# Two heads' context keys and values projected early, an inverse transform with two matrices, and a norm moved to ScalarE

## The chip, the core and the metric

The program runs on one core of one Trainium2 chip. A core has five engines that run at once, each with its own queue of instructions, and wait for each other by semaphores: TensorE (PE in the profile; its weight loads are PEld), VectorE (DVE), ScalarE (ACT), GpSimd (POOL) and SyncE (SP, which here only issues DMAs). The metric is the device time of one execution in microseconds (us); lower is better.

## What is computed

A decoder of two layers in fp32 on x of 8 batches x 128 tokens x 512 features, with a context of the same shape. Each of six steps adds to x and is followed by a layer norm. The steps that the change touches, cut to what matters:

```python
def _autocorrelation(Q=x, K=ctx, V=ctx):        # 8 heads of 64, L = 128
    corr = ifft(fft(q) * conj(fft(k))).real     # along the tokens, for each column
    w, idx = top_k(corr, 9); w = softmax(w)
    for i in range(9):
        g = minimum(idx[..., i] + pos, L - 1)   # shifted values, the last one repeated
        out = out + w[..., i] * take_along_axis(v, g)

def _L1_xattn_ref(latents=x, context=ctx, ...): # 32 query heads, 8 key heads of 128
    kv = concatenate([context, latents], axis=1)
    q = rms_norm(latents @ Wq); k = rms_norm(kv @ Wk); v = kv @ Wv
    out = softmax(q @ k.T / sqrt(128)) @ v
    return out @ Wo

x = _layernorm(x + _L0_attn_ref(x, w1, w2, b2, mask))      # masked dense, gelu
x = _layernorm(x + _autocorrelation(x, ctx, ctx))
x = _layernorm(x + _L0_ffn_ref(x, ...))                     # base product and routed adapters
x = _layernorm(x + _L1_attn_ref(x, ...))                    # state space mixer, 8 groups
x = _layernorm(x + _L1_xattn_ref(x, ctx, ...))              # cross attention
x = _layernorm(x + _L1_ffn_ref(x, ...))                     # product with adapters
```

## The kernel before, in words

x stays in SBUF as eight tiles of 128 x 512, one for each batch. Large products are made in three passes (`three_pass`, L269 to L273): each operand is split into a rounded high part, written by ACT (`..._hi`), and the rest, written by DVE or POOL (`..._lo`), and PE adds high x high, low x high and high x low. The order of the instructions on each engine is written out by hand; nothing is scheduled by a planner. All times below are from the start of the span.

**Masked dense, 0 to 58 us** (`stage_masked_dense`, L282). PE takes the batches in a row. Each goes on through DVE (bias, L366), ACT (gelu, L334), POOL (sum into x, L348), DVE (norm statistics), POOL (`norm_rstd`, L233 and L235) and DVE (`norm_apply`, L241). A barrier ends the stage.

**Autocorrelation, 58 to 190 us** (class `Autocorrelation`; its order on each engine stands in `stage_routed_mixer`). For batch b PE turns the weights of the nine taps (`turn_weights`, L540), waits for ACT's copy, transforms them (`transform`, L548 and L549), makes the correlation of batch b + 2 (`correlate`, L522, L523), the transforms of the values of b + 1 (`values`, L532, L533), turns x of b - 2 (L251), makes the inverse transform (`out`, L565: four full fp32 products, one for each of the four tiles that DVE made in `products`, L695) and the spectra of b + 3 (`spectra`, L508 to L514). DVE makes the four products and then picks the nine taps of b + 1 (`pick`, L649 to L679, which ends with `b_weights`). After the output of batch 5 PE goes on with `routed.base(0)`, the first product of the next stage, which needs the low parts `c_w_lo` that POOL makes at L627, one of four slices in each of the batches 2 to 5, behind that batch's `norm_rstd`.

**Routed product, to about 262 us**, then the **mixer** to about 1660 us.

**Cross attention, 1660 to 2510 us** (`stage_cross_attention`, L1760). Its 64 units are 8 key heads x 8 batches (unit n: head n // 8, batch n % 8). In one round PE does `attend(n)`, `turn_q(n+2)`, `project_kv(n+3)`, `turn_probs(n+1)`, `score(n+2)`, `project_q(n+3)`, `turn_k(n+3)` and `out(n)`. `project_kv` makes keys and values of one head together, 256 columns: 12 passes over the context (high and low parts `e_ctx_hi`, `e_ctx_lo`) and 12 over x (`XH`, `XL`). ACT evacuates them (`evac_kv`, L2055 and L2059), splits the turned probabilities (L2092), makes the exponentials (L2084), and in the rounds whose n % 8 is 0 to 3 it rounds two weights of the next head (L182) before it copies the output (L2097) and the turned queries (L2077). The last step is a product with adapters, to the end.

## Time and profile before

| what | value |
|---|---|
| median of 3 runs | 2551.83 us (2551.8 to 2552.94) |
| the profiled execution's own time | 2551.84 us |
| its span, first to last instruction | 2550.1 us |
| PE busy over the span | 2477.9 us (97%) |
| PE busy, 58 to 186 us | 113.82 of 128 us, granted clock 0.94 |
| PE busy, 1700 to 2400 us | 700 of 700 us, granted clock 1.00 |
| DVE, ACT, POOL busy, 1900 to 2000 us | 66.60, 58.15, 25.47 us |
| granted clock of PE, 156 to 161 us | 0.50 |
| DMA share of 16 engines, 1900 to 2000 us | 0.10 |

Busy is the time in which an engine works on an instruction; matmuls overlap, so the time from the start of one to the start of the next is what one costs. The granted clock is a share of full speed (1.00 is 2.4 GHz, 0.50 is 1.2 GHz). What an engine waits for stands in brackets behind an instruction in the trace.

### The profile page before, as it was taken

What the parts mean: (1) busy time and instruction counts of PE and PEld (TensorE: products, weight loads), DVE (VectorE), ACT (ScalarE), POOL (GpSimd) and SP (SyncE); (2) the same over time, 40 slices, a digit from 0 to 9 for tenths busy, and PEclk for the clock granted to TensorE, in tenths of its full rate; (3) what the DMA queues carried; (4) which work ended last, traced back from release to release, by engine and by line L of the source; (5) the groups of instructions that cost most, each with busy time, mean ns of one, the idle gap of its engine ahead of it and who ended that gap; (6) DMA issues with size and microseconds to landing.
All of it is one profiled execution on the core that took longest, in us unless ns stands there. A gap on an engine that the chain in (4) does not pass through costs nothing. (4 is left out here: it accounts for less than half of the span.)

```text
span 2550.1 us, 39113 instructions
## 1 busy us (share of the span) xinstructions
PE 2477.9 (97%) x14056; PEld 2033.2 (80%) x14056; DVE 1866.3 (73%) x2530; ACT 1122.6 (44%) x2660; POOL 1082.3 (42%) x890
## 2 busy tenths in 40 slices
PE   7989899999999999999999999899999999999999
PEld 4547788888888888888888887788888888888886
DVE  4877986886977968859869678656666666666675
ACT  2323343343443443433434433455656556555551
POOL 3012655645655655556566555632312223222123
PEclk8999999999999999999999999999999999999999
DMA  4000420321412303313213131110101001000100
GB/s 151 28 1 9 164 101 30 144 95 54 145 42 91 120 29 120 116 38 136 71 64 139 38 116 64 60 42 26 34 18 34 26 17 42 16 27 26 56 3 34
DMA packets 61554, 163.82 MB, mean 64 GB/s; under 512 B 8336, under 2 KB 8976, under 8 KB 52944
## 3 DMA queue, kind: packets, MB, share of 16 engines
q1 hardware_dynamic: 60144, 159.21, 18.2%
q8 instruction: 113, 1.85, 0.3%
q10 hardware_dynamic: 1248, 2.36, 0.3%
q14 instruction: 49, 0.40, 0.1%
HBM read 158.92 MB, written 2.62 MB: 63 GB/s over the span
## 5 line engine op out<-in xcount | busy, mean ns | idle before, releaser
L271 PE MATMUL pair<-XH,d_w_hi 128*128 128x512 f32 x1160 | 471.8, 407 | 2.8 <-DVE d_gated L1633 1.7
L272 PE MATMUL pair<-XL,d_w_hi 128*128 128x512 f32 x1160 | 460.3, 397 | 0.0
L273 PE MATMUL pair<-XH,d_w_lo 128*128 128x512 f32 x1160 | 459.7, 396 | 0.0
L1492 POOL TENSOR_TENSOR d_decay<-d_decay,d_cb 128x1024 f32<-128x1024 f32 x128 | 311.1, 2431 | 137.2 <-DVE d_decay L1610 137.2
L1610 DVE TENSOR_TENSOR_SCAN d_decay<-d_decay,m_delta 128x1024 f32<-128x1024 f32 x128 | 363.5, 2841 | 1.5 <-DVE d_dtg L1578 1.5
L1473 POOL TENSOR_TENSOR d_w_lo<-d_w,d_w_hi 128x512 fp32r<-128x512 f32 x144 | 188.6, 1312 | 268.1 <-ACT d_w_hi L1313 267.4
L271 PEld LDWEIGHTS pair<-XH,d_w_hi 128*128 128x128 f32 x1160 | 218.8, 189 | 60.1 <-issue 12.8
L1595 DVE SCALAR_TENSOR_TENSOR d_hs<-pair,d_conv,d_hs 128x1016 f32<-128x1016 f32 (+2 forms) x192 | 242.9, 1265 | 29.2 <-ACT d_hs L1338 24.7
L273 PEld LDWEIGHTS pair<-XH,d_w_lo 128*128 128x128 f32 x1160 | 218.7, 189 | 52.9
L272 PEld LDWEIGHTS pair<-XL,d_w_hi 128*128 128x128 f32 x1160 | 219.0, 189 | 47.1
L1497 POOL TENSOR_TENSOR d_gated_lo<-d_gated,d_gated_hi 128x512 fp32r<-128x512 f32 x128 | 173.4, 1357 | 159.1 <-ACT d_gated_hi L1357 159.1
L1338 ACT ACTIVATE d_hs<-pair,d_conv 128x1024 f32<-128x1024 f32 x64 | 77.1, 1205 | 357.0 <-PE pair L273 357.0
L2084 ACT ACTIVATE e_probs<-pair,e_nm,e_rq 128x256 f32<-128x256 f32 x256 | 141.1, 562 | 175.5 <-DVE e_nm L2289 175.5
L271 PE MATMUL pair<-d_wo_hi,d_gated_hi 128*128 128x512 f32 x512 | 207.4, 405 | 7.9 <-POOL d_gated_lo L1497 7.9
L273 PE MATMUL pair<-d_wo_hi,d_gated_lo 128*128 128x512 f32 x512 | 201.3, 393 | 0.0
L272 PE MATMUL pair<-d_wo_lo,d_gated_hi 128*128 128x512 f32 x512 | 199.7, 390 | 0.0
L2188 POOL TENSOR_TENSOR e_rq<-e_rq,mhalf 128x4 f32<-128x4 f32 x64 | 64.7, 1010 | 268.6 <-DVE e_rq L2271 268.6
L1357 ACT ACTIVATE d_gated_hi<-d_gated 128x512 fp32r<-128x512 f32 x128 | 80.0, 631 | 218.2 <-PE pair L273 197.1
L1638 DVE TENSOR_REDUCE d_sq_sum<-d_xdt 128x128 f32<-128x1024 f32 x64 | 128.3, 2005 | 63.2 <-ACT d_xdt L1364 63.2
L1345 ACT ACTIVATE d_hs<-d_hs 128x1024 f32<-128x1024 f32 x64 | 67.7, 1058 | 161.0 <-DVE d_hs L1595 161.0
L1192 PEld LDWEIGHTS pair<-d_decay,d_xdt 128*64 128x64 f32 x2048 | 112.1, 138 | 28.3 <-issue 28.3
L1192 PE MATMUL pair<-d_decay,d_xdt 128*64 128x128 f32 x2048 | 127.6, 278 | 5.2 <-POOL d_decay L1492 5.2
(280 smaller groups left out, 6032.4 us busy)
## 6 DMA issues: line engine op xcount, KB each, us to landing
d_decay<-token_decays SPq DMA_DIRECT2D x64, 1024.0 KB, 4.9
d_w<-in_L_w_groups SPq DMA_DIRECT2D x144, 256.0 KB, 2.7
e_w<-in_L_w_heads SPq DMA_DIRECT2D x80, 256.0 KB, 2.7
d_wo<-in_L_wo_groups SPq DMA_DIRECT2D x64, 256.0 KB, 4.9
X<-in_x SPq DMA_DIRECT2D x8, 256.0 KB, 10.3
b_ctx<-in_ctx SPq DMA_DIRECT2D x8, 256.0 KB, 12.0
e_ctx<-in_ctx_t SPq DMA_DIRECT2D x4, 512.0 KB, 6.5
out<-X SPq DMA_DIRECT2D x8, 256.0 KB, 2.0
```

The source lines that it names most:

```text
L271: pe.matmul(out, wh, xh, start=first, stop=False)
L272: pe.matmul(out, wh, xl, start=False, stop=False)
L273: return pe.matmul(out, wl, xh, start=False, stop=last)
L1192: last = pe.matmul(Y[e * PM:(e + 1) * PM, b * S:(b + 1) * S], XDT[:, b, e * PM:(e + 1) * PM], R[:, j % RSLOT, e, b * S:(b + 1) * S], start ...
L1357: act.activation(GH[:, x, :, :], GT[:, 4 * x:4 * x + 4, b * S:(b + 1) * S], ACT.Copy).then_inc(q["g_hi"], 1)
L1473: pool.tensor_tensor(WL[:, w, :, :], WR[:, w, :, :], WH[:, w, :, :].bitcast(F32), ALU.subtract).then_inc(q["w_split"], 1)
L1492: pool.tensor_tensor(r, r, GM_[:], ALU.mult).then_inc(q["scores"], 1)
L1497: pool.tensor_tensor(GL[:, x, :, :], GT[:, 4 * x:4 * x + 4, b * S:(b + 1) * S], GH[:, x, :, :].bitcast(F32), ALU.subtract).then_inc(q["g_l ...
L1595: v.scalar_tensor_tensor(dst[:, :, back:], src[:, :, :S - back], PC[:, n, KM - 1 - back:KM - back], dst[:, :, back:], ALU.mult, ALU.add).t ...
L1610: v.tensor_tensor_scan(r, r, m["DELTA"][:], 0.0, ALU.mult, ALU.add).then_inc(q["decay"], 1)
L1638: v.tensor_reduce(SQS[:, b % 2, :], SQ[:].rearrange("p j t -> p t j"), AX.X, ALU.add)\
L2084: act.activation(PR[:, n % 2, h, :], score_bank(h), ACT.Exp, bias=NM[:, n % 2, h:h + 1], scale=RQ[:, n % 2, h:h + 1], accum_out=SUM[:, n % ...
```

## The change

It does six things.

1. A class `KeysAhead` projects context keys and values of the heads 2 and 5 before the attention, in eight items of two batches (a half of an item is one batch: 12 passes of 256 columns). Items 0 and 1 (head 2, batches 0 to 3) stand on PE behind the last batch of the masked dense stage, item 2 behind `values(0)` of the autocorrelation, and the items 3 to 7 at its batches 0, 2, 3, 4 and 5: one half ahead of `turn_weights`, the other between it and `transform`. Weights and context (2.5 MB) are loaded in the first stage; ACT and POOL split them; ACT copies each item out of PSUM, and SP stores it to DRAM.
2. In the attention the 16 units of these heads leave out the 12 passes over the context. ACT issues two DMAs of 64 KB one unit ahead for each; the copy of the values, their low part and the scaling of the keys become two instructions of 128 columns where one of 256 stood.
3. `out` makes two products where it made four: POOL adds the first two of DVE's tiles and subtracts the last two (`parts`), and ACT writes a third copy of the values with its row 0 replaced (two instructions more in `values_copied`).
4. The norm of the autocorrelation is applied by ACT (`shifted`), with a shift that POOL makes, and no more by DVE.
5. The four slices of `c_w_hi` and `c_w_lo` are made two in each of the batches 2 and 3.
6. Tiles move: the products to the area of the mixer's weights, so that SP loads the first of these once the last `out` is done (it did so at the stage's start); the routed product's small tiles to another area.

```diff
 # stage_masked_dense: SP, ACT, POOL, PE
+                keys.weights(sp, 0)
+                keys.context(sp)
                 sp.wait_ge(next_in, 16 * (1 + NB))
+                for i in range(2):
+                    keys.store(sp, i)
...
+                    if b == 1:
+                        keys.w_hi(act, 0)
+                    if 2 <= b < 6:
+                        keys.c_hi(act, b - 2)
+                for i in range(2):
+                    keys.copy(act, i)
+                    for b in (2 * i + 4, 2 * i + 5):
+                        keys.c_hi(act, b)
...
                     if b:
                         norm_rstd(c, pool, s, b - 1)
+                    if b == 1:
+                        keys.w_lo(pool, 0)
+                    if 2 <= b < 6:
+                        keys.c_lo(pool, b - 2)
...
+                pe.wait_ge(first.lo, NB)
+                for i in range(2):
+                    for half in range(2):
+                        keys.project(pe, i, half)
 # Autocorrelation
     def out(self, pe, b):
-        for i in range(4):
-            pe.wait_ge(q["products"], 4 * b + i + 1)
-            last = pe.matmul(c.bank[7][:, :], f(M_AA + i), self.PR[:, i, :], start=i == 0, stop=i == 3)
+        for i in range(2):
+            pe.wait_ge(q["parts"], 2 * b + i + 1)
+            last = pe.matmul(c.bank[7][:, :], f(M_A + i), self.PT[:, i, :], start=i == 0, stop=i == 1)
...
     def values_copied(self, act, b):
+        act.activation(self.AV[:], c.bank[1][:, :], ACT.Copy).then_inc(q["uf_copied"], 1)
+        act.activation(self.AX[:], c.bank[1][:, :], ACT.Copy).then_inc(q["uf_copied"], 1)
+        act.activation(self.BV[:], c.bank[2][:, :], ACT.Copy, scale=self.REST[:, 0:1]).then_inc(q["uf_copied"], 1)
+        act.activation(self.AX[0:1, :], c.bank[2][0:1, :], ACT.Copy, scale=-1.0).then_inc(q["uf_copied"], 1)
+    def shifted(self, act, b):
+        act.activation(self.c.X[:, b, :], self.c.X[:, b, :], ACT.Identity, bias=self.SHIFT[:, b:b + 1],
+                       scale=self.c.rstd[:, b, :]).then_inc(self.s.normed, 1)
...
-        if b in (2, 3, 4, 5):
-            act.activation(nxt["WH"][:, b - 2, :], nxt["W"][:, b - 2, :], ACT.Copy).then_inc(q["next_hi"], 1)
+        for k in {2: (0, 1), 3: (2, 3)}.get(b, ()):
+            act.activation(nxt["WH"][:, k, :], nxt["W"][:, k, :], ACT.Copy).then_inc(q["next_hi"], 1)
+    def parts(self, pool, b):
+        for i, op in enumerate((ALU.add, ALU.subtract)):
+            pool.wait_ge(q["products"], 4 * b + 2 * i + 2)
+            pool.tensor_tensor(self.PT[:, i, :], self.PR[:, 2 * i, :], self.PR[:, 2 * i + 1, :], op).then_inc(q["parts"], 1)
 # stage_routed_mixer: PE, ACT, POOL
+                    item = {0: 3, 2: 4, 3: 5, 4: 6, 5: 7}.get(b)
+                    if item is not None:
+                        keys.project(pe, item, 0)
                     auto.turn_weights(pe, b)
+                    if item is not None:
+                        keys.project(pe, item, 1)
                     auto.transform(pe, b)
...
+                    if item is not None:
+                        keys.copy(act, item)
+                    if b == 0:
+                        keys.w_hi(act, 1)
+                    if b:
+                        auto.shifted(act, b - 1)
...
+                for b in range(4, NB):
+                    keys.c_lo(pool, b)
+                auto.parts(pool, 0)
+                keys.w_lo(pool, 1)
                 for b in range(NB):
-                    norm_rstd(c, pool, auto.s, b)
+                    auto.shift(pool, b)
+                    if b + 1 < NB:
+                        auto.parts(pool, b + 1)
                     auto.next_lo(pool, b)
 # stage_cross_attention: PE, ACT, DVE
                     for i, (hi, lo) in enumerate(((CH, CL), (c.XH, c.XL))):
+                        if i == 0 and kept(n) is not None:
+                            continue
...
+                def fetch(n):
+                        act.dma_start(KN[:, n % 2, 0, :], keys.kept[kept(n), n % NB, :, 0:HD]).then_inc(kept_in[n % 2], 16)
+                        act.dma_start(KEPT[:, n % 2, :], keys.kept[kept(n), n % NB, :, HD:]).then_inc(kept_in[n % 2], 16)
                 def evac_kv(n):
+                    if n < U - 1:
+                        fetch(n + 1)
...
-                    act.activation(VH[:, n % 3, :, :], side(KVB, 1), ACT.Copy).then_inc(q["v_hi"], 1)
+                    for at, source in sides(n, 1):
+                        last = act.activation(VH[:, n % 3, at, :], source, ACT.Copy)
+                    last.then_inc(q["v_hi"], 1)
```

The next pieces are the program's order on one engine, before and after. First PE in the autocorrelation, at the end of the spectra (b_ctx), the turn of the weights of batch 3 (b_weights) and their transform (b_weights_t). Before:

```order
L508 MATMUL pair<-X,b_dft 128x512
L513 MATMUL pair<-b_ctx,b_dft 128x512
L514 MATMUL pair<-b_ctx,b_dft 128x512
L540 MATMUL pair<-ident,b_weights 128x128 x4
L548 MATMUL pair<-b_weights_t,b_dft 128x512
L549 MATMUL pair<-b_weights_t,b_dft 128x512
```

After (L270 to L272 are the three passes, which repeat; k_w is the key and value weights of the kept head):

```order
L533 MATMUL pair<-b_ctx,b_dft 128x512
L270 MATMUL pair<-k_w_hi,e_ctx_hi 128x256
L271 MATMUL pair<-k_w_lo,e_ctx_hi 128x256
L272 MATMUL pair<-k_w_hi,e_ctx_lo 128x256
...
L561 MATMUL pair<-ident,b_weights 128x128 x4
L270 MATMUL pair<-k_w_hi,e_ctx_hi 128x256
L271 MATMUL pair<-k_w_lo,e_ctx_hi 128x256
L272 MATMUL pair<-k_w_hi,e_ctx_lo 128x256
...
L569 MATMUL pair<-b_weights_t,b_dft 128x512
L570 MATMUL pair<-b_weights_t,b_dft 128x512
```

One half of an item stands ahead of the turn, the other half in the place where PE waited for ACT's copy of the turned weights. Next POOL in the autocorrelation: the four slices `c_w_lo` (batches 2 to 5 before, 2 and 3 after) between the norm's `rstd`. Before:

```order
L627 TENSOR_TENSOR c_w_lo<-c_w,c_w_hi 128x512
L233 TENSOR_SCALAR rstd<-moments 128x1
L235 TENSOR_TENSOR rstd<-rstd,mhalf 128x1
L627 TENSOR_TENSOR c_w_lo<-c_w,c_w_hi 128x512
L233 TENSOR_SCALAR rstd<-moments 128x1
L235 TENSOR_TENSOR rstd<-rstd,mhalf 128x1
L627 TENSOR_TENSOR c_w_lo<-c_w,c_w_hi 128x512
L233 TENSOR_SCALAR rstd<-moments 128x1
L235 TENSOR_TENSOR rstd<-rstd,mhalf 128x1
L627 TENSOR_TENSOR c_w_lo<-c_w,c_w_hi 128x512
```

After:

```order
L671 TENSOR_SCALAR b_shift<-moments,rstd 128x1
L665 TENSOR_TENSOR b_parts<-b_products 128x512 x2
L682 TENSOR_TENSOR c_w_lo<-c_w,c_w_hi 128x512 x2
L232 TENSOR_SCALAR rstd<-moments 128x1
L234 TENSOR_TENSOR rstd<-rstd,mhalf 128x1
L671 TENSOR_SCALAR b_shift<-moments,rstd 128x1
L665 TENSOR_TENSOR b_parts<-b_products 128x512 x2
L682 TENSOR_TENSOR c_w_lo<-c_w,c_w_hi 128x512 x2
L232 TENSOR_SCALAR rstd<-moments 128x1
L234 TENSOR_TENSOR rstd<-rstd,mhalf 128x1
L671 TENSOR_SCALAR b_shift<-moments,rstd 128x1
L665 TENSOR_TENSOR b_parts<-b_products 128x512 x2
```

The slices have moved ahead by two batches, and two sums `b_parts` of each batch stand in the queue. Last ACT in a round of the attention that also rounds two weights of the next head (e_wq_hi, e_wo_hi). Before:

```order
L2055 ACTIVATE e_k_sq,e_rk<-pair 128x128 x2
L2059 ACTIVATE e_v_hi<-pair 128x256
L2092 ACTIVATE e_probs_t_hi<-pair 128x512 x2
L2084 ACTIVATE e_probs,e_sum<-pair,e_nm,e_rq 128x256 x4
L2064 ACTIVATE e_k_hi<-pair,e_norm_w 128x256
L2070 ACTIVATE e_q_sq,e_rq<-e_q 128x128 x4
L182 ACTIVATE e_wq_hi<-e_w 128x512
L182 ACTIVATE e_wo_hi<-e_w 128x512
L2097 ACTIVATE e_o_hi<-pair 128x512
L2077 ACTIVATE e_q_hi<-pair,e_norm_w 128x512
```

After, in a unit of a kept head (e_k_norm and e_kept are the tiles that the DMAs fill):

```order
L2233 DMA e_k_norm<-context_keys 128x128
L2234 DMA e_kept<-context_keys 128x128
L2245 ACTIVATE e_k_sq,e_rk<-e_k_norm 128x128
L2245 ACTIVATE e_k_sq,e_rk<-pair 128x128
L2249 ACTIVATE e_v_hi<-e_kept 128x128
L2249 ACTIVATE e_v_hi<-pair 128x128
L2283 ACTIVATE e_probs_t_hi<-pair 128x512 x2
L2275 ACTIVATE e_probs,e_sum<-pair,e_nm,e_rq 128x256 x4
L2255 ACTIVATE e_k_hi<-pair,e_norm_w 128x256
L2261 ACTIVATE e_q_sq,e_rq<-e_q 128x128 x4
L182 ACTIVATE e_wq_hi<-e_w 128x512
L182 ACTIVATE e_wo_hi<-e_w 128x512
```

The two DMA issues stand ahead of the evacuation of the keys, and the values are copied in two instructions.

## Rows read from the trace of the kernel before

**Rows 1.** PE in one unit of the attention; start, us, engine, line, op, out<-in, count
```profile
1999.89 1.04 PE L1919 MATMUL pair<-ident,e_probs 128*128 128x128 f32 x8
...
2009.76 0.37 PE L271 MATMUL pair<-e_wkv_hi,e_ctx_hi 128*128 128x256 f32 x1
...
2011.27 0.28 PE L271 MATMUL pair<-e_wkv_hi,XH 128*128 128x256 f32 x1
...
2012.71 1.04 PE L1919 MATMUL pair<-ident,e_probs 128*128 128x128 f32 x8
```

**Rows 2.** ACT in the same unit; [idle before <-releaser]
```profile
2000.10 0.28 ACT L2055 ACTIVATE e_k_sq<-pair 128x128 f32<-128x128 f32 x1 [2.12 <-PE pair L273]
...
2008.49 1.15 ACT L182 ACTIVATE e_wq_hi<-e_w 128x512 fp32r<-128x512 f32 x2
```

**Rows 3.** DVE in the same unit
```profile
2001.03 0.42 DVE L2247 TENSOR_TENSOR e_v_lo<-pair,e_v_hi 128x256 fp32r<-128x256 f32 x1
...
2011.03 0.73 DVE L2276 SCALAR_TENSOR_TENSOR e_q_lo<-pair,e_norm_w,e_q_hi 128x512 fp32r<-128x512 f32 x1
```

**Rows 4.** DMA issues of ACT at the program's start
```profile
0.81 1.87 ACTq L324 DMA_DIRECT2D a_w<-in_L_attn_w2t  x4
2.71 0.91 ACTq L325 DMA_DIRECT2D a_mask<-in_L_attn_sparse_mask  x1
```

**Rows 5.** PE from the first stage into the second
```profile
50.20 0.40 PE L273 MATMUL pair<-a_attn_hi,XL 128*128 128x512 f32 x1
58.53 2.04 PE L508 MATMUL pair<-X,b_dft 128*128 128x512 f32 x2 [7.93 <-PEq L92]
```

**Rows 6.** POOL in the first stage
```profile
35.98 0.23 POOL L233 TENSOR_SCALAR rstd<-moments 128x1 f32<-128x1 f32 x1 [0.75 <-DVE moments L227]
36.29 0.57 POOL L235 TENSOR_TENSOR rstd<-rstd,mhalf 128x1 f32<-128x1 f32 x1
```

**Rows 7.** DVE's last instruction of the first stage
```profile
56.99 0.55 DVE L241 TENSOR_SCALAR X<-X,moments,rstd 128x512 f32<-128x512 f32 x1 [0.75 <-POOL rstd L235]
```

**Rows 8.** PE in the autocorrelation, batch 0
```profile
75.11 1.13 PE L513 MATMUL pair<-b_ctx,b_dft 128*128 128x512 f32 x2 [1.66 <-ACT b_bv L589]
...
76.93 0.60 PE L540 MATMUL pair<-ident,b_weights 128*128 128x128 f32 x4
```

**Rows 9.** PE in the autocorrelation, batches 3 to 7
```profile
115.23 0.60 PE L540 MATMUL pair<-ident,b_weights 128*128 128x128 f32 x4
116.51 1.13 PE L548 MATMUL pair<-b_weights_t,b_dft 128*128 128x512 f32 x2 [0.69 <-ACT b_weights_t L606]
...
122.27 3.60 PE L565 MATMUL pair<-b_products,b_dft 128*128 128x512 f32 x8
...
128.28 0.60 PE L540 MATMUL pair<-ident,b_weights 128*128 128x128 f32 x4
...
148.39 3.60 PE L565 MATMUL pair<-b_products,b_dft 128*128 128x512 f32 x8
...
162.21 0.60 PE L540 MATMUL pair<-ident,b_weights 128*128 128x128 f32 x4
...
174.27 0.66 PE L540 MATMUL pair<-ident,b_weights 128*128 128x128 f32 x4 [0.58 <-DVE b_weights L679]
```

**Rows 10.** DVE in the autocorrelation, batch 3
```profile
118.53 0.69 DVE L695 TENSOR_TENSOR b_products<-b_av,pair 128x512 f32<-128x512 f32 x1 [0.26 <-PE pair L549]
...
126.55 0.69 DVE L679 TENSOR_TENSOR b_weights<-b_weights,b_rsum 128x512 f32<-128x512 f32 x1
```

**Rows 11.** POOL in the autocorrelation, batch 5
```profile
155.83 1.26 POOL L627 TENSOR_TENSOR c_w_lo<-c_w,c_w_hi 128x512 fp32r<-128x512 f32 x1
```

**Rows 12.** PE at the start of the routed product
```profile
191.67 0.33 PE L772 MATMUL pair<-ident,c_mid 128*128 128x128 f32 x1 [1.83 <-DVE c_mid L847]
```

**Rows 13.** two lines of DVE: count, duration min/median/max in ns
```profile
L2271 DVE TENSOR_SCALAR e_rq<-e_rq x64: 136/167/1069, 1664.5 to 2472.4; 128x4 f32<-128x4 f32 x64
L1610 DVE TENSOR_TENSOR_SCAN d_decay<-d_decay,m_delta x128: 2266/2720/4521, 267.8 to 1576.9; 128x1024 f32<-128x1024 f32 x128
```

More of the change, by code:

```diff
@@ L520, in correlate @@
             pe.wait_ge(q["corr_copied"], b)
+        if b >= 2:
+            pe.wait_ge(self.keys.q["copied"], 4 if b < 4 else b + 1)
         for j in range(4):
@@ L720, with __init__ @@
     RING, LOW, OUT, TURNED = (4, 5, 7), (1, 2), (3, 0), 6
-    def __init__(self, c, e, w, behind):
-        self.c, self.w, self.words, self.behind = c, w, 6 * D, behind
+    def __init__(self, c, e, w, behind, mid_t):
+        self.c, self.w, self.words, self.behind = c, w, 0, behind
         def at(name, shape):
-            tile = e.place("c_" + name, shape, F32, "decay", self.words)
+            tile = e.place("c_" + name, shape, F32, "kv", self.words)
             size = 1
@@ L755, in low @@
         if b < 2:
-            pe.wait_ge(self.behind.q["uf_copied"], 2 * NB - 1 + b)
+            pe.wait_ge(self.behind.q["uf_copied"], 4 * NB)
         else:
@@ L779, in base @@
             pe.wait_ge(self.behind.q["corr_copied"], NB)
+            pe.wait_ge(self.behind.keys.q["copied"], KeysAhead.ITEMS)
         elif b == 1:
@@ L872, in __init__ @@
         self.q = sems(c, "d0_", "in_ par_in mask delta one2 w_hi w_lo x_ready u abs exp one log inverse rest ratio "
-                                "dt a neg_a decay cut stored turned copied")
+                                "dt rates decay cut stored turned copied")
     def inputs(self, sp):
@@ L933, in decay @@
         q = self.q
-        act.wait_ge(q["neg_a"], 1)
+        act.wait_ge(q["rates"], 2)
         act.wait_ge(q["dt"], 1)
@@ L988, in copied, with stage_routed_mixer @@
                           self.c.bank[2 + h][:, :]).then_inc(self.q["copied"], 1)
-def stage_routed_mixer(c, loaded, w, m, w_groups, wo_groups, rows, e, a, low):
+def stage_routed_mixer(c, loaded, keys, w, m, w_groups, wo_groups, rows, e, a, low):
     nc = c.nc
@@ L1007, in stage_routed_mixer @@
         st.enter_context(nc.sbuf_tensor("d_late", [P, 16 * S + JT * D + 8], F32))
-        auto = Autocorrelation(c, loaded, w, e, late)
-        routed = RoutedLora(c, e, w, auto)
+        auto = Autocorrelation(c, loaded, w, e, late, keys)
+        routed = RoutedLora(c, e, w, auto, sb("c_mid_t", [P, 2, P]))
         steps = TokenSteps(c, m, e, low, a, rows.rearrange("g j (e t) -> (g j e) t", e=2))
@@ L1117, in _ @@
                 sp.sem_inc(preset, 1)
+                keys.weights(sp, 1)
+                for i in range(2, keys.ITEMS):
+                    keys.store(sp, i)
                 steps.inputs(sp)
+                sp.wait_ge(auto.q["out_ready"], NB)
                 for i in range(5):
@@ L1412, in _ @@
                 auto.spectrum(act, 2)
+                keys.copy(act, 2)
                 for b in range(NB):
                     auto.weights_turned(act, b)
+                    item = {0: 3, 2: 4, 3: 5, 4: 6, 5: 7}.get(b)
+                    if item is not None:
+                        keys.copy(act, item)
+                    if b == 0:
+                        keys.w_hi(act, 1)
+                    if b:
+                        auto.shifted(act, b - 1)
                     if b + 2 < NB:
@@ L1426, in _ @@
                 auto.hi(act, NB - 2)
+                auto.shifted(act, NB - 1)
                 routed.mid_turned(act, 0)
@@ L1757, in _, with stage_cross_attention @@
                     turned_lo(c, v, s, b, x_bank(b))
-def stage_cross_attention(c, e, a, result):
+def stage_cross_attention(c, e, a, result, keys):
     nc, q, ct = c.nc, e.q, e.ct
@@ L1830, in tokens, with kept, sides @@
             return slice((n % NB) * S, (n % NB + 1) * S)
+        def kept(n):
+            return keys.HEADS.index(n // NB) if 0 <= n < U and n // NB in keys.HEADS else None
+        KEPT = sb("e_kept", [P, 2, HD])
+        kept_in = [c.sem(f"e_kept_in{i}") for i in range(2)]
+        kept_order = [n for n in range(U) if kept(n) is not None]
+        def sides(n, kv):
+            if kept(n) is None:
+                return [(slice(0, 2), side(KVB, kv))]
+            first = KEPT[:, n % 2:n % 2 + 1, :] if kv else KN[:, n % 2, 0:1, :]
+            return [(slice(0, 1), first), (slice(1, 2), side(KVB, kv)[:, 1:2, :])]
         def ahead(eng, sem, count):
@@ L2050, in _ @@
             def _(act):
+                def fetch(n):
+                    if kept(n) is not None:
+                        ahead(act, "k_turned", n - 1)
+                        ahead(act, "v_lo", n - 1)
+                        act.dma_start(KN[:, n % 2, 0, :], keys.kept[kept(n), n % NB, :, 0:HD]).then_inc(kept_in[n % 2], 16)
+                        act.dma_start(KEPT[:, n % 2, :], keys.kept[kept(n), n % NB, :, HD:]).then_inc(kept_in[n % 2], 16)
                 def evac_kv(n):
+                    if n < U - 1:
+                        fetch(n + 1)
+                    if kept(n) is not None:
+                        act.wait_ge(kept_in[n % 2], 32 * (1 + sum(1 for o in kept_order if o < n and o % 2 == n % 2)))
                     act.wait_ge(q["kv_proj"], n + 1)
@@ L2054, in evac_kv @@
                     for i in range(2):
-                        last = act.activation(KSQ[:, i, :], KVB[:, i * KV:i * KV + HD], ACT.Square,
-                                              accum_out=RK[:, n % 2, i:i + 1])
+                        source = KVB[:, i * KV:i * KV + HD] if i or kept(n) is None else KN[:, n % 2, 0, :]
+                        last = act.activation(KSQ[:, i, :], source, ACT.Square, accum_out=RK[:, n % 2, i:i + 1])
                     last.then_inc(q["k_sq"], 1)
                     ahead(act, "o_ready", n - 2)
-                    act.activation(VH[:, n % 3, :, :], side(KVB, 1), ACT.Copy).then_inc(q["v_hi"], 1)
+                    for at, source in sides(n, 1):
+                        last = act.activation(VH[:, n % 3, at, :], source, ACT.Copy)
+                    last.then_inc(q["v_hi"], 1)
                 def k_hi(n):
@@ L2438, in program @@
                      ONE2=sb("m_one2", [P, 2]))
+            keys = KeysAhead(c, e, a, st, raw)
             low = -(-nc.sbuf_base // 32) * 32
```

180 lines of the change are left out of this document (133 added, 47 removed).

## The prediction

> **What bounds the kernel now.** I read the busy shares by stretch first, then the order of time on PE, ACT, DVE and POOL in one round of the attention, in one batch of the autocorrelation and across the end of the first stage. In the attention PE never stops: 700 of 700 us busy in the table above. One round lasts from one turn of the probabilities to the next, 1999.89 to 2012.71: 12.82 us [rows 1]. ACT waits 2.12 us in it for PE's key and value passes [rows 2]. So a pass that PE doesn't make is time gained there, until another engine's cycle becomes as long as PE's. The mixer (262 to 1660 us) keeps its instructions and is taken as unchanged. In the first stages PE is no longer full, and a chain over several engines decides.
>
> **Attention.** The 12 passes over the context run from 2009.76 to 2011.27, those over x from 2011.27 to 2012.71: 1.51 and 1.44 us [rows 1]. The first pass behind the fp32 turns starts slower, which the first pass over x then inherits, so 1.44 us go in each of 16 units: -23.0 us. PE's round becomes 11.38 us.
>
> Against it stands ACT. It now issues two DMAs a unit, ahead of the squares of the keys. ACT's issues at the start of the program took 1.87 us for four and 0.91 for one [rows 4], and ACT does nothing else meanwhile. For a 64 KB issue there is no row; the bounds are 0, if it hides in ACT's wait, and 0.91 us; I take 1.87 / 4 = 0.47, the row with the plainest shape, so 0.94 a unit. Splitting the copy of the values adds one short instruction, at most the 0.28 of a 128-column one [rows 2], less where they overlap. DVE's two splits cost 2 x 0.28 against 0.42 [rows 3], 0.14 each, and delay the maximum that ACT waits for by about as much; I count 0.28 for all splits together (bounds 0 and 0.6). In a round in which ACT also rounds two weights, its wait of 2.12 then becomes 2.12 - 1.44 - 0.94 - 0.28 = -0.54: ACT's cycle is 0.54 longer than PE's, and PE waits for the query's low part. There are 4 such rounds with a fetch for each kept head, 8 in all: +4.3 us. The first of them spends a reserve: the low part ends at 2011.76 [rows 3], the scores follow the turns of 2012.71, some 0.8 us long, so the reserve is 2013.5 - 2011.8 - 1.4 = 0.3, twice: -0.6. In the other rounds ACT lacks the 1.15 us of the two weights [rows 2] and has 0.6 to spare. The data land a unit ahead of their use, and the DMA engines are busy 0.10 there. Attention: -23.0 + 3.7 = -19.3 us.
>
> **Masked dense.** PE is idle from 50.6 to 58.53 [rows 5]; the four halves there are 4 x 1.44 = 5.8 us, hidden if their operands are ready. The price is on POOL, which stands in the chain of every batch. Its two rstd instructions take 35.98 to 36.86, 0.9 us [rows 6], a sum or a low part of 128 x 512 takes 1.26 [rows 11]. After 36.86 POOL has the low part of the weights (2 x 1.26 = 2.5), four rounds of sum, rstd and context part (3.4 to 3.5 each), two of sum and rstd (2.2), and the last rstd: 36.9 + 2.5 + 13.9 + 4.4 + 1.0 = 58.7, then DVE's last norm with its wait 0.6 + 0.3 = 59.6. Before, that norm ended at 57.54 [rows 7]. So +2.1 us (bounds 0 and 5: at 5 none of POOL's added 7.5 us but a third is covered). ACT's six copies behind the last gelu end at about 59 and hide. PE's clock has fallen to half in the long idle before; the new idle (56 to 61) is shorter, but I count nothing back.
>
> **Autocorrelation.** Batch 3 takes 115.23 to 128.28 = 13.05 us on PE, back to back but for 0.69 us of waiting for ACT's copy [rows 9]. The output loses half of 3.60 us, 1.7 net; the first half of an item adds 1.44, the second adds 1.44 - 0.69 = 0.75: 13.5 us. The chain weights turned, copied, transformed, products, next nine taps is 115.23 to 126.55 + 0.69 = 12.0 us [rows 9, 10]. POOL's `parts` now run beside the start of the pick. A DVE instruction on four columns took 167 ns at the median and 1069 at most [rows 13], the long ones beside POOL's work; so I add 0.5 us to the chain for the pick's two small ones (bounds 0 and 1.8): 12.5, or 13.25 with a second half in it. A batch takes the longer of the two:
>
> - 0, 1 and 2: 13.25 + 12.5 + 13.5 = 39.25, before 76.93 to 115.23 = 38.30 [rows 8, 9]: +0.95
> - 3: 13.5 for 13.05: +0.45
> - 4 and 5: 13.5 + 13.25 = 26.75, before 128.28 to 162.21 = 33.93: -7.2
> - 6: 12.5, before 162.21 to 174.27 = 12.06: +0.45
>
> The -7.2 is a stall. After the output of batch 5 (148.39 + 3.6 = 152.0) PE stood still until the last slice of c_w_lo was made, 155.83 + 1.26 = 157.1 [rows 9, 11], and then made the 12 passes of `base(0)` at half clock, to 162.21. With all slices made in batches 2 and 3, the passes start at once at full clock (about half of 5.1 us) and fit under the pick. Ahead of batch 0, item 2 (2.9 us) fills PE's wait of 1.66 [rows 8] and the first half of item 3 adds 1.44: +2.6. The two further copies on ACT (about 1 us) end before the pick wants its exponentials, by over a microsecond, and `parts` ends about when PE has done the values and the turn of x. At the end, output 7 comes 1.7 us earlier, ACT applies the norm, and DVE is free for the routing sooner; PE waited 1.83 us for it [rows 12], which I take back: -1.8. Together 2.6 - 5.35 - 1.8 = -4.5 us. Moving the first mixer weights behind the last output costs nothing: they are rounded some 20 us later.
>
> **Sum.** -19.3 + 2.1 - 4.5 = -21.7 us. The profiled execution took 2551.84 us (span 2550.1 and 1.7 around it), the median is 2551.83, so the forecast is 2530 us.
>
> One rule speaks against moving work to POOL. The long cases above are of a one-input instruction; the scan, which reads two tiles of SBUF, spread from 2266 to 4521 ns [rows 13], so such instructions suffer too. The Trainium skill (GPSIMD Engine Reference, Specifications) says the same of the interfaces to SBUF: shared with VectorE, with contention for instructions in a two-port mode or with two SBUF inputs. By that rule the five at the end of the pick would suffer where POOL's pairs reach so far; by my order POOL has finished 1 us before. The sum does not hang on it, rival 2 does.
>
> **Rivals.**
>
> 1. *The issues hide, and the early gain is larger.* ACT needs next to nothing for a 64 KB issue, or PE's reserve is larger than one row shows: the full 23.0. And with the stall gone the clock stays up at the start of the routed product: 1 to 3 us. Then 2551.8 - 23.0 - 2.4 - 2 = 2524 us. For it: ACT's wait is the only slack I count. Against it: the issues of rows 4.
> 2. *POOL becomes the bound of the early stages.* It gets about 45 us of work more before 190 us. If its pairs run beside the end of the pick, its last five instructions on DVE, together about 1.85 us (the last of them is the 0.69 of rows 10), double: 1.85 us in seven batches, 13 us, in place of my 0.5 x 7; with the first stage at its bound of 5 the time is 2530 + 9.5 + 3 = 2542 us. For it: the spread in rows 13. Against it: the idle of POOL, over 10 us a batch.
> 3. *ACT's queue holds the whole of the kept heads.* At 0.91 us an issue, ACT's cycle is 12.82 - 2.12 + 1.82 + 0.28 = 12.80 with the weights and 11.65 without: hardly a gain in 8 rounds, 1.2 in the other 8, so -9 in all; 2551.8 - 9.4 - 2.4 = 2540 us.
> 4. *Slower.* The same mechanism at a higher price, place `fetch` on ACT's queue. With an issue of d us the 8 rounds with weights change by 2d - 1.84 and the 8 others by 2d - 2.99 us. With the early -2.4 the change is above zero from 32d = 41.0, d = 1.28 us; no issue of ACT or SP in the trace took so long without waiting. At d = 1.5 it is +6.7: 2559 us.
>
> **Chances.** The forecast's own case 0.50 (2524.5 to 2536), rival 1 0.22, rival 2 0.14, rival 3 0.08, rival 4 0.03; the remaining 0.03 for a part that does not act as it says. Range 2519 to 2543: the low end is rival 1 with the splits free and 3 us of clock, the high end rival 2. This kernel's runs tell a change of 0.2%, 5.1 us, from none. Faster by more: 0.92; within it (2547 to 2557): 0.04; slower: 0.04.
>
> **What would show each step.** In the profile after: rounds of kept heads at about 11.4 us without weights and 12.0 with them, 12.82 elsewhere; ACT DMA issues near 0.47 us; PE waiting for DVE's query low part only in rounds with weights; the second stage starting near 60.7; turns of weights 13.5 us apart in batches 2 to 4; no wait of PE for c_w_lo; the turn of batch 6 some 4 us earlier after the stage's start than before. The prediction is wrong if the rounds of kept heads stay at 12.8, if the first stage ends after 63, or if the pick grows by more than 1 us.

## The result, and the profile after

| | median us | runs |
|---|---|---|
| before | 2551.82 | 4, 2550.58 to 2552.94 |
| after | 2532.52 | 4, 2531.31 to 2534.21 |

The ratio is 0.9925, 95% interval 0.9908 to 0.9942: 19.3 us faster, where 21.7 was forecast. The profiled span is 2531.0 us, before 2550.1.

PE in the early stages, after (start, us, engine, line; the last column is the idle time and its releaser), which answers to [rows 5, 8, 9, 12]:

```profile
60.76 2.05 PE L527 MATMUL pair<-X,b_dft 128*128 128x512 f32 x2 [4.53 <-PEq L92]
...
81.86 0.60 PE L561 MATMUL pair<-ident,b_weights 128*128 128x128 f32 x4
...
95.07 0.66 PE L561 MATMUL pair<-ident,b_weights 128*128 128x128 f32 x4 [1.67 <-DVE b_weights L734]
96.41 2.07 PE L569 MATMUL pair<-b_weights_t,b_dft 128*128 128x512 f32 x2 [0.69 <-ACT b_weights_t L639]
...
109.32 0.66 PE L561 MATMUL pair<-ident,b_weights 128*128 128x128 f32 x4
...
135.99 0.66 PE L561 MATMUL pair<-ident,b_weights 128*128 128x128 f32 x4
...
162.54 0.66 PE L561 MATMUL pair<-ident,b_weights 128*128 128x128 f32 x4 [0.85 <-DVE b_weights L734]
...
175.16 1.11 PE L561 MATMUL pair<-ident,b_weights 128*128 128x128 f32 x4 [1.51 <-DVE b_weights L734]
...
190.36 1.10 PE L928 MATMUL pair<-c_b,c_mid_t 128*128 128x512 f32 x2 [2.32 <-ACT c_mid_t L945]
...
191.73 0.27 PE L905 MATMUL pair<-ident,c_mid 128*128 128x128 f32 x1
```

The second stage starts at 60.76 (58.53 before). The stall is gone: batches 4 and 5 take 162.54 - 135.99 = 26.55 us (33.93 before). But the second c_mid comes at 191.73, before at 191.67, and the last of the eight at 229.19 and 229.16: all that was gained early was also spent early. Batch 1 stands out with 14.25 us, its first transform at half clock (2.07 for 1.13).

VectorE in the pick, on four columns: before; after; and GpSimd's two sums of that batch:

```profile
121.84 0.17 DVE L654 TENSOR_SCALAR b_negmax<-b_max 128x4 f32<-128x4 f32 x1
```

```profile
129.72 0.67 DVE L709 TENSOR_SCALAR b_negmax<-b_max 128x4 f32<-128x4 f32 x1
```

```profile
127.85 2.51 POOL L665 TENSOR_TENSOR b_parts<-b_products 128x512 f32<-128x512 f32 x2 [2.60 <-DVE b_products L749]
```

The instruction ends at 130.39, GpSimd's second sum at 130.36. It takes 0.66 to 0.68 us in seven of the eight batches after, and 0.17 in all eight before.

In the attention a round of PE (one turn of the probabilities to the next) takes 12.81 us as before, and in each kept head six of 11.38 to 11.55, then 11.68, 11.74 and one of 14.15 (14.14 in the second head). This ninth round is the first that makes all 24 passes again, and without a delay it would take 12.81. PE, after, around it:

```profile
1937.45 1.04 PE L2096 MATMUL pair<-ident,e_probs 128*128 128x128 f32 x8
...
1948.67 0.36 PE L270 MATMUL pair<-e_wkv_hi,e_ctx_hi 128*128 128x256 f32 x1 [0.74 <-DVE e_k_lo L2453]
1951.60 1.04 PE L2096 MATMUL pair<-ident,e_probs 128*128 128x128 f32 x8
```

The nine rounds of the first kept head sum to 106.08 us against 9 x 12.81 = 115.3: 9.2 gained, 18.6 with the second. The first turn of the probabilities stands 0.65 us earlier than before (1679.50, 1680.15), and 18.6 + 0.65 is the result. The 0.65 was not gained in the early stages: the last c_mid turn is no earlier than before. It lies in the mixer, whose instructions are the same; from that turn to the first turn of the probabilities the kernels shown here take 1450.3 to 1451.7 us.

ScalarE, after, in a kept round with weights. The issues run beside its copies, and it still waits for PE:

```profile
1901.04 0.60 ACT L2288 ACTIVATE e_o_hi<-pair 128x512 fp32r<-128x512 f32 x1
1901.46 0.33 ACTq L2233 DMA_DIRECT2D e_k_norm<-context_keys  x1
1901.52 0.69 ACT L2268 ACTIVATE e_q_hi<-pair,e_norm_w 128x512 fp32r<-128x512 f32 x1
1901.82 0.46 ACTq L2234 DMA_DIRECT2D e_kept<-context_keys  x1
1902.88 0.31 ACT L2245 ACTIVATE e_k_sq<-e_k_norm 128x128 f32<-128x128 f32 x1 [0.68 <-PE pair L272]
```

VectorE, after, in the round ahead of PE's wait of 0.74 us:

```profile
1936.20 1.07 DVE L2465 TENSOR_SCALAR e_rq<-e_rq 128x4 f32<-128x4 f32 x1
...
1940.16 1.38 DVE L2446 TENSOR_TENSOR e_k_norm<-e_k_norm,e_rk 128x128 f32<-128x128 f32 x1 [0.92 <-POOL e_rk L2374]
1941.46 0.28 DVE L2446 TENSOR_TENSOR e_k_norm<-pair,e_rk 128x128 f32<-128x128 f32 x1
```

GpSimd at the same time:

```profile
1935.95 2.54 POOL L187 TENSOR_TENSOR e_wo_lo<-e_w,e_wo_hi 128x512 fp32r<-128x512 f32 x2 [7.58 <-ACT e_wo_hi L182]
1938.44 1.03 POOL L2379 TENSOR_TENSOR e_rq<-e_rq,mhalf 128x4 f32<-128x4 f32 x1
1939.44 0.69 POOL L2374 TENSOR_TENSOR e_rk<-e_rk,mhalf 128x2 f32<-128x2 f32 x1
1940.11 2.59 POOL L187 TENSOR_TENSOR e_wkv_lo<-e_w,e_wkv_hi 128x512 fp32r<-128x512 f32 x2
```

The half of the keys that comes from SBUF takes 1.38 us, the half from PSUM 0.28. The 1.38 ends where the first of GpSimd's two e_wkv_lo (1.3 us each) ends. Of the 1.33 us that the round is too long, 0.37 has come by the scores, ahead of this, and 0.96 comes at the wait of 0.74 (counted against the same round of experiment 12).

### The profile page after: what moved, and what is told of

Its sections match the earlier page's. It is cut to its first block and busy times, and to the rows that moved or that the text cites. A ratio compares the mean times of both kernels' runs of the same rounds, so it can differ in the third digit from the quotient of the medians.

```text
span 2531.0 us, 39264 instructions
## 1 busy us (share of the span) xinstructions
PE 2463.3 (97%) x14024; PEld 2024.7 (80%) x14024; DVE 1869.2 (74%) x2554; ACT 1148.7 (45%) x2718; POOL 1120.1 (44%) x926
## 5 line engine op out<-in xcount | busy, mean ns | idle before, releaser
L270 PE MATMUL pair<-XH,d_w_hi 128*128 128x512 f32 x1160 | 471.6, 407 | 2.8 <-DVE d_gated L1798 1.7
L272 PE MATMUL pair<-XH,d_w_lo 128*128 128x512 f32 x1160 | 459.5, 396 | 0.0
L270 PEld LDWEIGHTS pair<-XH,d_w_hi 128*128 128x128 f32 x1160 | 218.7, 189 | 60.1 <-issue 12.8
L272 PEld LDWEIGHTS pair<-XH,d_w_lo 128*128 128x128 f32 x1160 | 218.5, 188 | 52.9
L270 PE MATMUL pair<-d_wo_hi,d_gated_hi 128*128 128x512 f32 x512 | 207.2, 405 | 7.9 <-POOL d_gated_lo L1655 7.9
L272 PE MATMUL pair<-d_wo_hi,d_gated_lo 128*128 128x512 f32 x512 | 201.2, 393 | 0.0
```

The source lines that it names most:

```text
L270: pe.matmul(out, wh, xh, start=first, stop=False)
L272: return pe.matmul(out, wl, xh, start=False, stop=last)
```

## The experiments

Times are medians; "mixer" is the start of the last c_mid turn ahead of it on PE (229.16 before, 229.19 after), a mark for all that was gained or lost early. It is read from one execution. In the changed kernel and the experiments 7, 8, 9 and 11, whose early stages are the same, the second stage starts at 60.45 to 61.51 and the mark stands at 228.62 to 230.72, 168.2 to 169.2 behind that start; smaller differences of marks show nothing.

### The early stages

**1. Slices alone.** Before, with

```diff
-        if b in (2, 3, 4, 5):
+        for k in {2: (0, 1), 3: (2, 3)}.get(b, ()):
```

in `next_hi` and `next_lo`.

> The kernel before with one part of the change alone: the four slices of c_w_hi and c_w_lo made in batches 2 and 3. Theory (the stall): PE no longer stands still from 152.0 to 157.1 us, base(0) runs at full clock, and the turn of the weights of batch 6 comes 7 to 8 us earlier, at 154 to 155 us; the time is 2544 to 2546 us. Rival (given back): the routed product's start hangs on another chain, PE's idle only moves to 175 to 190 us and its clock falls there; batch 6 comes earlier, the mixer's start at most 3 us, and the time is 2549 to 2551 us.

2544.22 us (ratio 0.9969, 0.9957 to 0.998), -7.1. Batch 6 at 154.42 for 162.21, mixer 221.62, 7.5 earlier: the gain is carried through. The rival falls.

**2. Slices back.** After, with the first line again, and `next_lo(b)` ahead of `parts(b + 1)` on GpSimd. (Behind it the sums of batch 6 would wait for PE, PE for the slice, and the slice for the sums.)

> The changed kernel with the slices back in batches 2 to 5, each ahead of the sums of the next batch on GpSimd. Theory (the stall): it comes back whole, batches 4 and 5 take 33 to 35 us in place of 26.55, and the time is 2538 to 2541 us against 2532.5. Rival: with the key items in batches 4 and 5 PE has work of its own and the stall is largely covered: +0 to +3 us, 2532.5 to 2535.5.

2542.18 us, +9.7 over the changed kernel: batches 4 and 5 take 35.6 us, mixer 237.52. That is over both forecasts; the slice also stands ahead of the next batch's sums here, so this is not the stall alone. The key items don't cover it.

**3. No items.** After, without the eight items and the fetches:

```diff
-                        keys.project(pe, item, 0)
...
-            return keys.HEADS.index(n // NB) if 0 <= n < U and n // NB in keys.HEADS else None
+            return None
```

> The changed kernel without the eight items and with all 24 passes in every unit of the attention: inverse transform with two matrices, norm on ScalarE and slices stay. Theory: the second stage starts at 58.5 again, a batch of the autocorrelation takes 12.1 to 12.6 us, the attention's rounds are 12.82 throughout; the items cost some 7 to 8 us ahead of the attention, and 18.6 are gained in it, so this kernel is at 2543 to 2545 us. Rival: the items are nearly free in the holes (under 3 us) and the rest of the change is worth nothing: 2548 to 2551 us.

2549.43 us (0.9991, 0.9982 to 1.0001). The rival's time, and its price of the items: the rest of the change is worth nothing on balance. But that is a gain and a loss of one size. Against experiment 1 the two matrices and the norm cost 5.2 us (5.0 by the marks), about what the slices bring; the items, with 16 x 1.44 = 23 us of work on PE, cost 2.6 (mixer 226.59 to 229.19), 1.9 of it at the second stage's start, near what marks can show. PE of this kernel:

```profile
76.70 1.49 PE L512 MATMUL pair<-b_ctx,b_dft 128*128 128x512 f32 x2 [2.70 <-ACT b_av_cross L595]
77.98 1.91 PE L513 MATMUL pair<-b_ctx,b_dft 128*128 128x512 f32 x2
79.69 1.06 PE L539 MATMUL pair<-ident,b_weights 128*128 128x128 f32 x4
...
106.70 0.66 PE L539 MATMUL pair<-ident,b_weights 128*128 128x128 f32 x4 [1.25 <-DVE b_weights L712]
108.04 2.08 PE L547 MATMUL pair<-b_weights_t,b_dft 128*128 128x512 f32 x2 [0.69 <-ACT b_weights_t L617]
109.91 1.80 PE L548 MATMUL pair<-b_weights_t,b_dft 128*128 128x512 f32 x2
...
121.00 0.66 PE L539 MATMUL pair<-ident,b_weights 128*128 128x128 f32 x4 [1.05 <-DVE b_weights L712]
...
148.55 0.66 PE L539 MATMUL pair<-ident,b_weights 128*128 128x128 f32 x4 [1.37 <-DVE b_weights L712]
149.90 1.13 PE L547 MATMUL pair<-b_weights_t,b_dft 128*128 128x512 f32 x2 [0.69 <-ACT b_weights_t L617]
```

Two things: ahead of batch 0 the added copies of ScalarE hold PE (2.70 for 1.66 [rows 8]), and from then on PE, with less to do, waits twice in a batch, and in batches 1, 2 and 4 it goes on at half clock (granted 0.51 in the transform of batch 2). There the transform, 3.5 us for 1.9, stands on the chain from one pick to the next, and the batch takes 14.05 to 14.62 us. Batches 3, 5 and 6 have waits of much the same length, but full clock behind them (149.90 above), and take 12.6 to 12.9. The waits of one batch don't tell which it will be. The table of stretches (stretch, length; busy us of PE, weight loads, VectorE, ScalarE, GpSimd; granted clock, DMA share, GB/s):

```profile
58.00:110.00 52.00, 42.91 (x137) 22.34 (x138) 33.42 (x132) 19.96 (x40) 9.00 (x18) 0.86 0.13 42
```

The same stretch before, and in the changed kernel:

```profile
58.00:110.00 52.00, 46.98 (x172) 25.82 (x173) 38.61 (x151) 18.05 (x37) 4.59 (x11) 0.95 0.17 57
```

```profile
58.00:110.00 52.00, 46.04 (x196) 28.29 (x197) 32.68 (x131) 21.09 (x41) 16.18 (x22) 0.90 0.17 56
110.00:160.00 50.00, 50.00 (x248) 33.47 (x248) 45.96 (x169) 29.31 (x59) 20.52 (x25) 1.00 0.10 32
```

**4. One step of ScalarE.** After, with `mid_turned(0)` and `exp(1)` ahead of `shifted(7)`.

> The changed kernel with one step of ScalarE moved: the copy of c_mid_t of batch 0 and the exponential of batch 1 stand ahead of the norm of batch 7, not behind it. Theory: PE's wait of 2.32 us for c_mid_t ahead of the first close goes, the second c_mid turn comes at 190.7 in place of 191.73, and the mixer starts about 1 us earlier: 2531.5 us. Rival: each of the following batches hangs on VectorE's routing, which is not earlier; the wait moves and the time stays at 2532.5.

2533.21 us. The first close comes at 187.90 (190.36 after) and the second c_mid at 191.13, yet the mixer's mark is 229.05, 0.14 us earlier, as is the second stage's start by 0.20. The rival holds.

**5. Two matrices alone.** Experiment 3 with the norm on VectorE.

> The kernel of experiment 3 (no items, full attention) with the norm back on VectorE: the inverse transform with two matrices and the slices alone. Theory (clock): PE has 3.6 us less in each batch, waits for the chain weights, transform, products, pick, its clock falls in the wait, and the transform of the weights, which stands on that chain, takes 3.5 us in place of 1.9; the norm has no part in it, so the time stays near that of experiment 3: 2548 to 2551 us. Rival: the norm on ScalarE (0.81 us ahead of its other copies) and its three steps on GpSimd lengthen the chain: without it the time is that of the slices alone, 2543 to 2545 us.

2548.48 us, mixer 226.75 (226.59 with the norm on ScalarE): 0.95 us less by the medians, 0.16 more by the marks, so the norm's move can't be told from nothing. The two matrices alone make the kernel of experiment 1 slower by 4.3 us.

**6. Filler.** Experiment 3 with

```diff
+                    if b:
+                        auto.filler(pe, b)      # one fp32 product of 128x512, not read
                     auto.turn_weights(pe, b)
+                    if b:
+                        auto.filler(pe, b)
```

> The kernel of experiment 3 with PE work added that nobody reads: one fp32 product of 128x512 (0.86 us) ahead of the turn of the weights and one between turn and transform, in batches 1 to 7, 12 us in all. Theory (clock): the clock stays up, the transform takes 1.9 us everywhere, every batch 12.6 to 12.8 us, and a kernel that does more work is 4 to 6 us faster than experiment 3: 2543.5 to 2545.5 us. Rival (the chain of VectorE, ScalarE and GpSimd is what has grown, whatever PE does): no change, 2549 us, or up to 12 us slower.

2544.21 us, 5.2 less than experiment 3, with 12 us more work on PE. At the place shown above:

```profile
104.26 0.66 PE L539 MATMUL pair<-ident,b_weights 128*128 128x128 f32 x4 [0.65 <-DVE b_weights L715]
105.61 1.11 PE L547 MATMUL pair<-b_weights_t,b_dft 128*128 128x512 f32 x2
106.56 1.02 PE L548 MATMUL pair<-b_weights_t,b_dft 128*128 128x512 f32 x2
...
116.88 0.66 PE L539 MATMUL pair<-ident,b_weights 128*128 128x128 f32 x4 [0.20 <-DVE b_weights L715]
```

Batches are 12.5 to 12.9 us, and the granted clock is 1.00 in each transform. So the loss of experiment 3 against experiment 1 is PE's clock on the chain: with the filler the two matrices are level with the four (2544.21 and 2544.22 us). They are not ahead, for a batch without waits at half clock is still bound by that chain, 12.6 us with the 0.5 us of b_negmax in it. The items are such a filler that does useful work: in the changed kernel the five batches with an item run their transforms at full clock.

### The attention

**7. One wait on GpSimd.** After, with

```diff
+                    if keys_in(n):
+                        pool.wait_ge(q["k_norm"], n + 4)
                     for m in keys_in(n) + weights_in(n):
                         e.w_lo(pool, m)
```

> The changed kernel with one wait added on GpSimd: the low parts of the next head's key and value weights start only when VectorE has scaled the keys of that unit. It changes nothing in VectorE's or PE's order. Theory (contention): the scaling of the kept keys (both inputs in SBUF) takes 0.3 us in place of 1.38, PE's wait of 0.74 us for the keys' low part goes, and the round of 14.15 us in each kept head falls to 12.9 to 13.1: 2530.2 us. Rival (queue): the round is long since GpSimd is late with e_rk behind the other weights' low parts, and since ScalarE's fetch and split come ahead; it stays at 14.1, and the time at 2532.5.

2531.37 us (profiled span 2529.4 for 2531.0); the long rounds are 13.18 and 13.17. VectorE of this kernel:

```profile
1940.61 0.29 DVE L2448 TENSOR_TENSOR e_k_norm<-e_k_norm,e_rk 128x128 f32<-128x128 f32 x1 [0.91 <-POOL e_rk L2374]
```

The hold of 1.09 us is gone and the rounds are 0.97 shorter, a little less than forecast. The remaining 0.37 us is lost ahead of the scores; I put it down to the other weights' low parts, which still make GpSimd late with e_rk (0.91 us of waiting as before), and experiments 9 and 12 bear that out. In the medians 1.2 us is within what two sets of runs differ by; the rounds show it plainly.

**8. Fetches issued by SyncE**, in the order of its loads.

> The changed kernel with the 16 pairs of fetches issued by SyncE, between its loads of weights, and none by ScalarE. Theory: ScalarE's issues (0.33 + 0.46 us a unit) run beside the end of its copies and hide in its wait for PE, so the rounds of kept heads stay at 11.39 us, the two of 11.68 and 11.74 too, for there VectorE and GpSimd are late: 2532.5 us, at best 1 us less. Rival (my forecast's term): ScalarE's cycle bounds the rounds with weights; the rounds of 11.55 to 11.74 fall to 11.38 and the 14.15 by as much as the issues took, 0.8 us: 2529.5 us.

2532.46 us. Rounds of 11.65 to 11.76 and 14.15, 14.12 stay; the one of 11.55 goes to 11.40. But it is 11.39 in experiments 7 and 11 too, where ScalarE issues. No cost of the issues can be seen.

**9. All low parts later.** Each pair of low parts behind the next unit's `k_norm`.

> The changed kernel with the low parts of the next head's weights moved on GpSimd, all of them: each pair stands behind the next unit's e_rk and starts only when VectorE has scaled that unit's keys, in place of the start of the next round. Theory (GpSimd's place beside VectorE and its lateness are all that is left in the kept heads): e_rq and e_rk are no longer late, VectorE's e_rq takes 0.16 us in place of 1.07, the rounds of 11.68, 11.74 and 14.15 us become 11.4, 11.4 and 12.8 to 12.9: 3.9 us less over the two heads, 2528.6 us. Rival: the same amount of GpSimd's work now runs beside VectorE's low parts of the probabilities and the maxima, which are on the way to the scores and grow: no gain over the one wait of experiment 7, 2531 us or slower.

2532.82 us: both are right in part. Rounds of 11.68 and 11.74 become 11.39 and 11.40, but once in every head but the last a round grows by 0.6 to 0.8 us, where four low parts stand in a row: 12.82 to 13.44, 11.39 to 12.02, or the long one, which is 13.58 and not 12.82. GpSimd, then VectorE:

```profile
1747.02 2.55 POOL L187 TENSOR_TENSOR e_wo_lo<-e_w,e_wo_hi 128x512 fp32r<-128x512 f32 x2 [0.54 <-DVE e_k_norm L2449]
1749.53 2.55 POOL L187 TENSOR_TENSOR e_wkv_lo<-e_w,e_wkv_hi 128x512 fp32r<-128x512 f32 x2
```

```profile
1736.55 0.22 DVE L2486 SCALAR_TENSOR_TENSOR e_nm<-e_mx,e_rq 128x4 f32<-128x4 f32 x1
...
1749.85 0.99 DVE L2486 SCALAR_TENSOR_TENSOR e_nm<-e_mx,e_rq 128x4 f32<-128x4 f32 x1
```

e_nm, on four columns and ahead of the exponentials, is held until 1750.8.

**10. With filler.** Experiment 9, with the filler in batches 1 and 7 and 33 passes of 256 columns behind the items of the first stage.

> Experiment 9 with filler on PE in the three idle places of the early stages where the changed kernel's clock is at half afterwards: 33 passes of 256 columns (3.9 us) behind the items of the first stage, and two fp32 products in each of the batches 1 and 7 (of the kind of experiment 6); nobody reads them. Theory (clock): the second stage's first products run at full speed (5.06 us become 2.9), the transforms of batches 1 and 7 take 1.9 in place of 3.6 us; batch 1 gives 1.6, the start 2, batch 7 at most 1.5: 3.5 to 5 us less than experiment 9, 2524 to 2525.5 us. Rival: what is gained at the start is lost in the chain over VectorE and ScalarE that follows, as at the routed product, and at most 1.6 us remains: 2527 us.

2528.74 us, 4.1 less. The second stage starts at 61.32, 0.6 later than after, but at full clock: batch 0's turn is at 80.01 (81.86 after), batch 1 takes 12.62 us (14.25), and from the turn of batch 7 to the mixer's mark it is 51.48 us (54.03). The mark is 223.11, 6.1 earlier than after and 7.6 earlier than in experiment 9. The medians give only 4.1: the traces are of the longest execution of experiment 9 (2534.88 us) and the shortest of this one (2527.27). The three fillers were not tried one by one.

**11. One tensor input.** After, with the kept half as `tensor_scalar` (a scalar for each partition).

> The changed kernel with the kept half of the keys scaled by an instruction with one tensor input and a scalar for each partition, in place of one with two tensor inputs in SBUF. Theory (it is the second input in SBUF that makes it wait for GpSimd): 0.2 to 0.4 us in place of 1.38, the round of 14.15 falls to about 13.1, the time 2530.5 us. Rival (any instruction of VectorE whose input is in SBUF can be held as long as a GpSimd instruction runs, as e_rq on four columns was, 1.07 us): 1.2 to 1.5 us, the round stays at 14.1, the time at 2532.5.

2531.98 us, rounds 14.09. VectorE and GpSimd:

```profile
1939.41 1.31 DVE L2448 TENSOR_SCALAR e_k_norm<-e_k_norm,e_rk 128x128 f32<-128x128 f32 x1 [0.91 <-POOL e_rk L2374]
```

```profile
1939.35 2.54 POOL L187 TENSOR_TENSOR e_wkv_lo<-e_w,e_wkv_hi 128x512 fp32r<-128x512 f32 x2
```

The rival holds: it is held all the same, until 1940.7.

**12. The best.** Experiment 10 with three of the four pairs later and never four low parts together.

```diff
+                    if n % NB in (1, 2, 3) and weights_in(n - 1):
+                        pool.wait_ge(q["k_norm"], n + 4)
+                        for m in weights_in(n - 1):
+                            e.w_lo(pool, m)
+                    if n % NB == 3:
+                        for m in weights_in(n):
+                            e.w_lo(pool, m)
```

> Experiment 10 with at most two low parts behind a unit's scaled keys: three of a head's four pairs one unit later, the fourth where the changed kernel has it, the key and value pair behind the one wait of experiment 7. Theory (four low parts in a row, 5.1 us of GpSimd, hold VectorE's e_nm, 0.99 us for 0.22, once in each head): the rounds of 13.44 us go back to 12.82 and that of 12.02 to 11.39; in the kept heads one round of 11.74 is left or none, and the long one is 12.9 to 13.2. Five or six rounds of 0.62 and two of 0.63 us go: 2528.7 - 5 = 2523.7 us. Rival (the extra rounds come from weights that are ready too late for PE or from the DMA ring of four, not from GpSimd's hold on VectorE): they stay or move to another unit, 2527 to 2529 us.

2523.75 us (0.9888, 0.9872 to 0.9905), as forecast: 8.8 us under the changed kernel, 28 under before. The eight kept rounds are 11.38 to 11.48, those of the other heads 12.81 or 12.82, but for the first and the last few, which are as before, and the long one is 12.82 too. PE's first product of the second stage:

```profile
61.92 1.10 PE L531 MATMUL pair<-X,b_dft 128*128 128x512 f32 x2 [0.97 <-PEq L92]
```

## Why the prediction was right, and where it was not

The time was right within 2.5 us, in part by luck: two terms failed, and other causes of about their size stood in their place. By its steps:

- **Attention, -19.3; measured -18.6.** The size was right and its second term was not; that the two agree within 0.7 us is luck. The passes are worth 12.81 - 11.39 = 1.42 us, as worked out. The term "ACT's cycle is 0.54 longer than PE's", +3.7 us in eight rounds, did not come: the issues take 0.33 and 0.46 us but run beside a copy (after's ScalarE rows), and without them nothing changes (experiment 8). In its place stand 1.33 us in one round and 0.65 in two more of each head, 4.0 us in all (a 0.16 in one round of the first head comes and goes from trace to trace): VectorE held by GpSimd, and GpSimd late, in the units where the next head's low parts are made. Experiments 7 and 9 take away the one and the other, and 12 both. So rival 2's mechanism was at work in the attention, where I had not looked for it.
- **Masked dense, +2.1; measured +2.2.** Right: GpSimd is without a wait from 36.71 to 57.89, its last rstd ends at 59.19 (58.7 forecast) and VectorE's norm at 59.77 (59.6). The start of the second stage differs by 1 us between traces.
- **Slices, -7.2; measured -7.1 in experiment 1**, batches 4 and 5 at 26.55 us (26.75 forecast). Right.
- **The pick, +0.5 a batch; measured +0.5**, b_negmax at 0.67 for 0.17 beside GpSimd's sums, and in two of the picks another 0.3 in b_ninth, beside c_w_lo. Right, in size and cause. The last five instructions of the pick kept their times, so rival 2 did not come there.
- **Ahead of batch 0, +2.6; measured +2.7, for another reason.** Without any item it is 20.82 us from the stage's start for 18.40 (experiment 3): the copies on ScalarE, which I took to end before they matter, hold PE by 1.04 us more, and the clock falls in that wait (the first product behind it takes 1.49 us for 1.13, the second 1.91). The items came at next to nothing.
- **Batches 0 to 2, +0.95; measured 40.77 - 38.30 = +2.5.** Batch 1 has no item, so PE lacks work there and takes the transform at half clock. I had set its chain at 12.5 us; experiment 6 shows 12.6 for it, at full clock. What failed is that the chain's own length was taken as independent of what PE does in its waits. (Batches 3 and 6 took 13.36 and 12.62, near their 13.5 and 12.5.)
- **Routed end, -1.8; measured -0.86**, from the turn of batch 7 to the mixer's mark (54.03 us for 54.89). PE's wait of 1.83 for c_mid is gone, but one of 2.32 for c_mid_t, behind the norm, stands there; without it the mark hardly moves (experiment 4). Half clock at batch 7 takes nothing from before, where it was the same (the transform is 3.57 us for 3.48); it is what experiment 10 wins back. What holds the later turns was not tried.
- **Mixer, 0; measured -0.68**, within what its time varies by from one trace to another.

So the early sum was -2.4 and came out at 0.03 at the mixer's mark and at -0.65 at the attention's start. Two figures of the prediction don't follow from its own numbers: at d = 1.5 rival 4 gives +7.0 and not +6.7, and the low end of 2519 lies 4 below what is said of it. And rival 4 says that no issue was as long as 1.28 us, but three of SyncE's before took 1.46, 1.89 and 2.67 us; whether they waited for anything the trace doesn't say. Of the change's parts the attention brings 18.6 and the slices 7; the two matrices lose 5, and the items, with the first stage's later end, 2.6. What the changed kernel would do with four products and the items was not tried.

The Trainium skill (SBUF — State Buffer, "SBUF: two separate sides") calls the pair of ports that VectorE and GpSimd share an exclusive lock, held for the whole instruction by whichever starts first: a GpSimd instruction, or one of VectorE in a two-port mode or, against a GpSimd instruction that reads SBUF, with two inputs in SBUF. The traces agree as to the lock: 1.38, 1.31, 1.07 and 0.99 us, all starting behind GpSimd's instruction of 1.3 and ending with it. In which mode VectorE ran those with one tensor input no run here shows.

## What to carry to other kernels

Work moved into the holes of an engine costs little, and may pay twice: where TensorE's waits let its clock fall ahead of a step that stands on the chain, filler alone gave 5.2 us back. Removing TensorE's work from a stage that a chain bounds can make it slower (4.3 us in experiment 5), so look at the granted clock and at the duration of the first matmul behind each wait before counting the gain. When operands move from PSUM to SBUF, look what GpSimd runs beside the instruction that reads them.

## What the runs showed of the hardware

- A VectorE instruction with its inputs in SBUF was held up to 1.1 us beside a GpSimd `tensor_tensor` of 128x512, down to four columns (1.07 us for 0.16) and with one tensor input or two; with an input in PSUM it took 0.28 us beside the same instruction.
- Waits of 1.25 and 0.69 us with 0.66 us of work between them were followed by half clock (2.08 us for 1.11, experiment 3, batch 2), waits of 1.37 and 0.69 in the same kernel by full clock (batch 5); with 0.86 us of filler in each, every batch was at full clock.
- A 64 KB DMA issue took 0.33 or 0.46 us on ScalarE's queue, in part beside a running copy, and landed 1.8 or 2.1 us later (medians of 16).
